# Sending the last self-attention heads out in two halves of the rows, in a one-core transformer layer

## The reference, cut to what matters

```python
xn1 = _ln(x, g1, be1)
sa = _mha(xn1, xn1, Wq_s, ..., causal=True)      # 16 heads of 16 channels
x = x + (sa @ W1 + b1)
xn2 = _ln(x, g2, be2)
ca = _mha(xn2, encoder_out, Wq_c, ..., causal=False)   # 77 keys
x = x + (ca @ W2 + b2)
xn3 = _ln(x, g3, be3)
return x + relu(xn3 @ Wf1 + bf1) @ Wf2 + bf2
```

## Time and profile before

| | us |
|---|---|
| median of 3 runs (590.23 to 590.74) | 590.23 |
| profiled execution | 590.62 |
| its span | 588.7 |

### The profile page before, as it was taken

How to read it: one execution, slowest core, us unless ns; L and a number is a source line. 1 busy time by engine, 2 the same in 40 slices (tenths; PEclk the granted TensorE clock), 3 DMA queues, 4 the chain that set the end, 5 groups by cost and what they waited for, 6 DMA issues and landing times.

```text
span 588.7 us, 8826 instructions
## 1 busy us (share of the span) xinstructions
PE 486.3 (83%) x3296; PEld 283.9 (48%) x3296; DVE 335.5 (57%) x645; ACT 316.0 (54%) x622; POOL 189.5 (32%) x291
## 2 busy tenths in 40 slices
PE   1588974999999999989988888685359697999887
PEld 1475651343434444444433243441226177888877
DVE  3165885877878787867863054254625285363340
ACT  3685320667676767645566667264034981445360
POOL 2497970121212121221322333216511192030200
PEclk9998997999999999989999899787559987999999
DMA  8145946025253435340121944316741520101001
GB/s 285 56 135 177 223 126 110 0 37 94 57 99 65 76 64 100 65 68 3 34 59 55 195 112 79 75 40 186 123 92 23 137 68 0 37 1 37 19 18 37
DMA packets 31370, 48.12 MB, mean 82 GB/s; under 512 B 8928, under 2 KB 25824, under 8 KB 29408
## 3 DMA queue, kind: packets, MB, share of 16 engines
q1 hardware_dynamic: 31260, 47.54, 34.9%
q10 hardware_dynamic: 68, 0.02, 0.0%
HBM read 30.66 MB, written 12.03 MB: 73 GB/s over the span
## 4 chain that ended last, share of the span: by engine, by line
PE 56%; DVE 12%; DMA 10%; ACT 10%; SPq 3%; issue 3%; POOL 2%; ACTq 0%; DVEq 0%
PE ps L1227 12%; PE ps L1075 11%; PE ps L1143 9%; PE ps L1196 9%; PE ps L1308 6%; DVE max_a L1385 4%; ACT arena_p L943 4%; PE ps L1165 4%; DMA stacks<-qc_parts 3%; DMA recips<-recip_rows 3%; PE ps L1061 2%; DVE hid_r L1488 2%; PE ps L1182 2%; PE ps L1147 2%; ACT xn L986 2%
## 5 line engine op out<-in xcount | busy, mean ns | idle before, releaser
L943 ACT ACTIVATE arena_p<-ps 128x512 f32<-128x512 f32 (+4 forms) x416 | 191.1, 543 | 151.6 <-PE ps L1196 150.7
L1385 DVE TENSOR_REDUCE max_a<-ps 128x1 f32<-128x512 f32 (+4 forms) x280 | 158.6, 620 | 70.8 <-PE ps L1143 58.7
L1143 PE MATMUL ps<-stacks 96*128 96x77 bf16 (+4 forms) x640 | 138.4, 291 | 31.1 <-DVE max_a L1385 11.3
L1196 PE MATMUL ps<-stacks 99*128 99x512 bf16 (+1 forms) x448 | 140.9, 346 | 19.1 <-DMA stacks<-shift_t 8.6
L1143 PEld LDWEIGHTS ps<-stacks 96*128 96x128 bf16 x640 | 55.0, 105 | 95.6 <-DVE max_a L1385 38.7
L1227 PE MATMUL ps<-arena_p,v_group 128*32 128x512 f32 (+3 forms) x896 | 92.9, 527 | 0.3 <-POOL arena_p L807 0.3
L807 POOL TENSOR_SCALAR_AFFINE_SELECT arena_p<-arena_p 128x512 f32<-128x512 f32 x64 | 39.9, 635 | 161.5 <-ACT arena_p L943 161.4
L1196 PEld LDWEIGHTS ps<-stacks 99*128 99x128 bf16 x448 | 42.0, 99 | 80.7 <-ACT arena_p L943 36.2
L1385 DVE TENSOR_REDUCE max_b<-ps 128x1 f32<-128x384 f32 (+3 forms) x88 | 52.9, 636 | 22.4 <-PE ps L1147 22.1
L1075 PE MATMUL ps<-wf2r,hid_r 128*128 128x256 f32 x384 | 47.1, 284 | 4.9 <-DVE hid_r L1488 3.8
L746 POOL TENSOR_TENSOR xs<-xs,row 128x256 f32<-128x256 f32 x48 | 39.6, 859 | 33.3 <-DVE xn L1342 33.3
(11 more groups left out here) (79 smaller groups left out, 505.0 us busy)
## 6 DMA issues: line engine op xcount, KB each, us to landing
arena_h<-out_t SPq DMA_DIRECT2D x16, 256.0 KB, 4.5
recips<-recip_rows SPq DMA_DIRECT2D x8, 512.0 KB
q_parts<-parts SPq DMA_DIRECT2D x8, 384.0 KB, 2.6
k_parts<-parts SPq DMA_DIRECT2D x8, 384.0 KB, 2.9
stacks<-q_parts SPq DMA_DIRECT2D x7, 384.0 KB, 5.5
stacks<-k_parts SPq DMA_DIRECT2D x7, 384.0 KB, 7.8
qc_parts<-parts SPq DMA_DIRECT2D x6, 384.0 KB, 3.5
stacks<-qc_parts SPq DMA_DIRECT2D x6, 384.0 KB, 6.8
```

The lines of the kernel that those rows point to most:

```text
L943: nc.scalar.activation(probs[0:a.kp, a.probs_slot(g, ui), h, k * BANK:k * BANK + width], ps[0:a.kp, unit % S_BANKS, 0:width], ACT.Exp, sca ...
L1143: ins = nc.tensor.matmul(m_bank(use)[:, o:o + w], q_columns(a, g, ROWS, h, t * P, (t + 1) * P), k_self[0:ROWS, slot, h, s0:s0 + w] if a.causal
L1196: ins = nc.tensor.matmul(ps[:, unit % S_BANKS, lo - k * BANK:hi - k * BANK], k_rows(a, ROWS_S, g, h, i * P), q_columns(a, g, ROWS_S, h, q0 ...
L1385: nc.vector.tensor_reduce(dst, m_bank(use)[:, 0:nh * w].rearrange("p (h w) -> p h w", h=nh), AX.X, ALU.max).then_inc(use_read, 1)
```

## The change

Self group 7 leaves in two halves of 512 rows. Piece 3 of its product, which completes bank 6, moves from -2.84 to -5.0; the first copy follows at -4.5, its DMAs at -4.0; the second copy is at +2.4 behind the last piece at +2.0 (was +2.9). Each half has its own reciprocal, store, spread (256 KB) and division, with four new semaphores; the halves of `sums` are laid out apart, so group 6's sums go by two DMAs. The rest of the list is laid anew: rows of chunk 2 come at +10 and of chunk 3 at +16, each with its own norm, turn and projection; loads, "packed", "bias", and "inverted" and "spread" of C3 get other places, "weights" becomes two steps behind the chunks of C4 and C5, and all that stood from +58 on stands 15 earlier.

```diff
+BANK_DONE = 3
+    early = ("product", SELF, NG - 1, BANK_DONE)
+    events = [(END - 5.0, 2, early) if e[2] == early else e for e in events]
-    crossed = [END + t for t in (0.0, 6.5, 13.5, 20.1, 58.0, 64.5, 74.0, 80.5)]
+    crossed = [END + t for t in (0.0, 6.5, 13.5, 20.1, 43.0, 49.5, 59.0, 65.5)]
-    add(END + 2.9, "product", SELF, NG - 1, SELF.n_pieces - 1)
+    add(END + 2.0, "product", SELF, NG - 1, SELF.n_pieces - 1)
+    for half, copied, inverted, divided in ((0, -4.5, 0.5, 7.0), (1, 2.4, 7.1, 15.0)):
+        add(END + copied, "copy", SELF, NG - 1, half)
+        add(END + copied + 0.5, "packed", SELF, NG - 1, half)
+        add(END + inverted, "inverted", SELF, NG - 1, half)
+        add(END + inverted + 0.1, "stored", SELF, NG - 1, half)
+        add(END + inverted + 0.1, "spread", SELF, NG - 1, half)
+        add(END + divided, "divided", SELF, NG - 1, half)
+    copied = {(1, 1): END + 16.5, (3, 0): END + 28.5, (3, 1): END + 30.0}
+    packed = {1: END + 16.6, 2: END + 27.2, 3: END + 30.1}
-    add(END + 51.9, "inverted", CROSS, 3)
-    add(END + 53.4, "spread", CROSS, 3)
-    add(END + 67.0, "divided", CROSS, 3)
+    for g, inverted, spread, divided in ((1, 17.5, 17.7, 31.9), (3, 39.0, 44.0, 52.0)):
+        ...
-    for n, t in enumerate([5.2 * SELF_US, 5.8 * SELF_US, END + 17.0, END + 17.1]):
+    for n, t in enumerate([5.2 * SELF_US, 5.8 * SELF_US, END + 10.0, END + 16.0]):
...
-        add((t + 6.0, t + 6.0, END + 18.0, END + 19.0)[n], "norm", SELF, n)
-    for n, t in enumerate([6.25 * SELF_US, 6.6 * SELF_US, END + 21.0, END + 23.0]):
+        add((t + 6.0, t + 6.0, END + 13.0, END + 19.0)[n], "norm", SELF, n)
+    for n, t in enumerate([6.25 * SELF_US, 6.6 * SELF_US, END + 15.2, END + 21.5]):
...
-            add(t + 3.0 + 1.0 * hh, "qproj", SELF, n, hh)
-            add(t + 5.0 + 1.0 * hh, "second", SELF, n, hh)
-    for n, t in enumerate([END + 9.0, END + 13.0, END + 32.0, END + 32.1]):
+            add(t + (3.0 if n < 2 else 2.2) + 1.0 * hh, "qproj", SELF, n, hh)
+            add(t + (5.0 if n < 2 else 4.2) + 1.0 * hh, "second", SELF, n, hh)
+    for n, t in enumerate([END + 8.0, END + 12.0, END + 28.0, END + 28.1]):
         add(t, "bias", SELF, n)
-    for g, half, t in ((4, 0, 27.5), (5, 0, 28.5), (4, 1, 31.5), (5, 1, 31.55), (6, None, 31.6), (7, None, 53.5)):
+    for g, half, t in ((4, 0, 21.0), (5, 0, 21.1), (4, 1, 27.0), (5, 1, 27.1), (6, None, 30.2), (7, None, 38.4)):
-    w2 = END + 70.0
+    w2 = END + 55.0
-    add(END + 32.2, "weights", SELF, 0)
-    add(END + 75.0, "raw", SELF, 0)
+    add(END + 36.6, "weights", SELF, 0)
+    add(END + 42.6, "weights", SELF, 1)
+    add(END + 60.0, "raw", SELF, 0)
@@ pack_sums; pack_heads takes lo:hi of the rows in the same way
+            if a.causal and g >= NG - 2:
+                for k in range(2) if half is None else [half]:
+                    eng.dma_start(sums_half[r0:r0 + GW, k, :],
+                                  out_t[1::2 * D, g % 2, k * CHUNK:(k + 1) * CHUNK]
+                                  .rearrange("h (s c) -> h s c", c=sums_half.shape[2]))\
+                        .then_inc(s.late_sums if half else s.sums_in[g % 2], 16)
+                return
@@ spread_recips
+                sp.dma_start(recips[:, lo:hi],
+                             src.rearrange("h (o t) -> h o t", o=1).to_broadcast([2 * GH, D, hi - lo]))\
+                    .then_inc(s.late_recips if half else s.recips_in, 16)
@@ copy_out
+                halves = a.n_copies if g < NG - 1 else 2
+                act.wait_ge(pv, a.pieces_to(g, BANK_DONE + 1 if a.causal and halves == 2 and n == 0
+                                            else (n + 1) * a.n_pieces // halves))
@@ rows (PE)
-                pe.wait_ge(of[a].heads_done, KC * (b + 1))
+                pe.wait_ge(of[a].heads_done, KC * (b + 1) + (a.causal and n == 3))
@@ divide_heads
+                lo, hi = (0, T) if half is None else (half * CHUNK, (half + 1) * CHUNK)
+                o = heads_out[:, g // 2, lo:hi]
+                nc.vector.tensor_tensor(o, o, recips[:, lo:hi], ALU.mult).then_inc(s.heads_done, 1)
```

More of the change, by code:

```diff
@@ L212, in add @@
         events.append((t, 3, what))
-    add(END + 2.9, "product", SELF, NG - 1, SELF.n_pieces - 1)
[L215 to L218, removed]
-        if g % 2:
[L220 to L224, removed]
+    add(END + 2.0, "product", SELF, NG - 1, SELF.n_pieces - 1)
+    for g in range(NG - 1):
+        after = starts[g + 1]
+        add(after + 5.4, "copy", SELF, g, 0)
+        add(after + 5.5, "packed", SELF, g, None)
+        if g % 2:
+            add(after + 10.1, "inverted", SELF, g, None)
+            add(after + 10.2, "stored", SELF, g, None)
+            add(after + 10.2, "spread", SELF, g, None)
+            add(after + 18.9, "divided", SELF, g, None)
+    for half, copied, inverted, divided in ((0, -4.5, 0.5, 7.0), (1, 2.4, 7.1, 15.0)):
[5 more added lines that the diff above has]
+        add(END + divided, "divided", SELF, NG - 1, half)
     for g in range(NG):
@@ L335, in build @@
         sums = sb("sums", [P, 2 * GH * T // P])
+        sums_half = sums[:, :].rearrange("p (k c) -> p k c", k=2)
         n_qkv, n_ctx = KC * 3 * C, KC * 2 * C
@@ L818, in attention @@
                         add_bias(NCH + what[0])
+                    elif op == "weights" and what[0] == 0:
+                        pool.wait_ge(ff_in, 16)
+                        pool.tensor_copy(wf1r[0], wf1).then_inc(wf1_halves, 1)
                     elif op == "weights":
-                        pool.wait_ge(ff_in, 16)
-                        weight_halves(*wf1r, wf1, wf1_halves)
+                        pool.wait_ge(wf1_halves, 1)
+                        pool.tensor_tensor(wf1r[1], wf1, wf1r[0], ALU.subtract).then_inc(wf1_halves, 1)
                     elif op == "second":
@@ L1217, in product @@
                     else:
[L1218 removed]
+                        pe.wait_ge(of[a.before].out_copied, NG * a.before.n_copies + 1)
                 slot = a.probs_slot(g, ui)
@@ L1408, in rows, with invert_sums, divide_heads @@
                     ln_sums(norm)
-            def invert_sums(a, g):
-                for p in range(2):
-                    dve.wait_ge(of[a].sums_in[p], 16 * (g // 2 + 1))
-                nc.vector.reciprocal(sums[:, :], sums[:, :]).then_inc(of[a].recips_done, 1)
-            def divide_heads(a, g):
-                dve.wait_ge(of[a].recips_in, 16 * (g // 2 + 1))
-                for p in range(2):
-                    dve.wait_ge(of[a].heads_in[p], 16 * (g // 2 + 1))
-                o = heads_out[:, g // 2, :]
-                nc.vector.tensor_tensor(o, o, recips[:, :], ALU.mult).then_inc(of[a].heads_done, 1)
+            def invert_sums(a, g, half=None):
+                if half:
+                    dve.wait_ge(of[a].late_sums, 16)
+                else:
+                    for p in range(2):
+                        dve.wait_ge(of[a].sums_in[p], 16 * (g // 2 + 1 + (half == 0 and p == 0)))
+                to = sums[:, :] if half is None else sums_half[:, half, :]
+                nc.vector.reciprocal(to, to).then_inc(of[a].recips_done, 1)
+            def divide_heads(a, g, half=None):
+                s = of[a]
+                if half:
+                    dve.wait_ge(s.late_recips, 16)
+                    dve.wait_ge(s.late_heads, 16)
+                else:
+                    dve.wait_ge(s.recips_in, 16 * (g // 2 + 1))
+                    for p in range(2):
+                        dve.wait_ge(s.heads_in[p], 16 * (g // 2 + 1))
+                lo, hi = (0, T) if half is None else (half * CHUNK, (half + 1) * CHUNK)
+                o = heads_out[:, g // 2, lo:hi]
+                nc.vector.tensor_tensor(o, o, recips[:, lo:hi], ALU.mult).then_inc(s.heads_done, 1)
             def attention(lo, hi=None):
```

79 lines of the change are left out of this document (46 added, 33 removed).

## The result

The changed kernel takes **587.57 us** (median of 6 runs, 586.54 to 588.23), beside 591.19 (590.23 to 593.77) of the kernel before: a ratio of 0.9931 [0.9906, 0.9956]. It is faster, by 3.6 us and not by the 12.9 of the forecast, and the time lies outside the range of 571 to 585. The profiled execution took 586.54 us (span 584.6) against 590.62.

A forecast was written before the change was run, and what follows sets the result against it. PE's waits behind the q projections, ended by landings of q parts, sums and q stacks, were taken as the bound. Savings of 2.3 + 3.2 + 2.9 - 1.5 + 6.0 = 12.9 us gave 577.3 us, range 571 to 585.

The forecast's parts named there:

- Rows, norm and projection: Chunk 2 and 3 rows up to the store of their parts: store 2.3 us earlier, 3 lost to 6 won.
- Arriving: First half's store 2.3 us and 256 KB spread 5.0 us after self attention: divided by 366.3; second half at 374.4.
- Weights behind the split: POOL's "weights" moved behind C4's split, so the split can follow its last maximum at once: 3.2 us won.
- Shift's copy: DVE's copy of C4's shift moved ahead of "inverted C3", which waited for sums: 2.9 us won.
- Load 6: Before C4's first score: issued at 412.6, lands 8.2 us later at 420.8; takes back 1.5 us, 0 to 4.8.
- Load 7: Issued earlier, behind C4's shift, so C4's first product no longer waits for it: 6.0 us won, or 3.3.
- Spread C3: Spread of C3's reciprocals, behind load 7 and C5's shift on SP, lands at 431.5: cost 0, up to 3.
- Feed-forward: Behind C4's first product all goes unchanged in the old order: 31.4 us, then feed-forward 117.6 us.
- signs of being wrong: Load 6 landing after 424, a wait for spread C3 over 3 us, or a longer feed-forward.
- The void halves: Rival: half a spread takes nearly as long as the whole; 580.0, or 582.6 with 3 us lost; chance 0.14.
- The DMA bound: Rival: DMA engines bound the stretch behind 403; load 6 takes 11.5 us, 5 lost together, 582.3; chance 0.17.
- The slower rival: Rival: first spread, behind load C3 on its queue, lands late and holds DVE and PE; 593 if at 382; chance 0.04.

The follow-up runs named there:

- after_warm: Changed kernel plus useless fp32 products on PE, 3 ahead of C3's third chunk step and 5 ahead of turn 2: 584.91 us, 0.9916.
- rows3_early: Changed kernel with the second half's division and chunk 3's rows moved ahead of norm 2 and turn 2: 591.07 us, 0.9985.
- halves_fixed_warm: Changed kernel with rows3_early, norm 3 ahead of the splits, first C4 and C5 loads behind the parts' stores, useless products at three places: 581.66 us, 0.9867.
- norm2_first: Changed kernel with norm 2 moved from +13 to +10.06, ahead of C3's last maxima and C3's split: 589.70 us, 0.9988.
- halves_reordered: Changed kernel with rows3_early, norm 3 ahead of the splits, and the second-half loads of C4 and C5, load 6, load 7 and spread C3 moved: 593.87 us, 1.0042.
- head_only: Changed kernel with the halves kept but the new order behind the store of the parts undone: 596.11 us, 1.0103 against the kernel before.
- tail_load7_late: tail_only with load 7 on SP behind the spread of C3, so also behind C5's shift: 590.51 us, 1.001.
- the second part: The change's new order behind the store of the parts, without the halves; alone on the kernel before: 581.79 us, 0.9864.
- tail_only: Kernel before with only the new order behind the store of the parts, group 7 leaving whole: 581.79 us, 0.9864.
- tail_load6: tail_only with load 6 ahead of packed C2 and C3, load 7 behind C3's reciprocals' store, spread C3 ahead of C5's shift: 587.25 us, 0.9913.
- piece3_back: Changed kernel with piece 3 of group 7's product behind the last exponentials again and the first copy at -2.3: 587.95 us, 0.9954.

## Why the prediction failed

**The step that failed is "Rows, norm and projection"**: the store of chunk 3's parts was to come 2.3 us earlier, between 3 lost and 6 won; it came 4.9 later, outside its bounds. That is 7.2 of the 9.6 us by which the stage misses the 12.9. By the forecast's own marks (what is off grows along the way; the changed kernel's trace runs 0.8 us ahead of that of the kernel before, so in R each is 0.8 later still):

| mark | forecast | measured |
|---|---|---|
| first half inverted, divided | 358.4, 366.3 | 358.42, 366.58 |
| rows of chunk 2 | 367.7 to 371.2 | 368.84 to 373.69 |
| norm 2, turn 2 | 378.8, 380.2 | 381.05, 382.57 |
| rows of chunk 3 | 382.4 to 385.9 | 386.83 to 391.16 |
| chunk 3's projection | 396.0 | 402.72 |
| store | 403.1 | 409.59 |

- *Arriving* was right, in part by luck. The store of the reciprocals took 3.33 us for 2.3, the spread of 256 KB 4.42 for 5.0, and the two nearly cancel. The forecast had taken 5.0 as a middle, from no row; that half the bytes take little more than half of 7.71 us bears it out. The Trainium skill (DMA: Bandwidth & Descriptors, "Anatomy of one DMA — SWDGE (gpsimd) path") puts a fixed 2.0 us and the bytes at 436 GB/s; by that, an estimate, half the spread saves 0.6 us. The trace has 3.3, so the measurement decides against using it here. That section fits DMAs of the path that GpSimd serves, and this spread is issued by SyncE, on the queue that the profile calls hardware_dynamic: no run here tests the fit on its own path.
- *PE's clock.* The forecast priced both "rows" at the full-clock 1.89 us per half and booked 1.1 us as won, since it read the block before as run at half clock. That reading was wrong: behind its wait the block ran at the lower level only for its first 2.9 us.

```profile
375.70:378.60 2.90, 2.90 (x7) 2.34 (x8) 0.00 (x0) 0.00 (x0) 0.00 (x0) 0.50 0.12 13
378.60:384.40 5.80, 5.80 (x28) 4.89 (x27) 3.74 (x11) 0.00 (x0) 0.72 (x2) 0.98 0.00 0
```

  That loss, some 1.1 us for the whole, is now met twice: the halves put a wait ahead of the first rows and a second, behind norm 2, ahead of turn 2. Rows 2, turn 2, C3's product (1.94 us for 1.06) and rows 3 cost 1.3, 0.9, 0.9 and 0.8 us more. That the clock does this is shown by `after_warm`, where norm 3 comes 4.0 us earlier. Its store, though, came only 1.3 us earlier, so the clock of these steps by itself does not bring the forecast's 2.3 us back.
- *Order on DVE.* Norm 3 was seen to stand behind both splits, and got no price of its own. It took 3.16 us where norm 2 took 1.38, beside POOL's 2.31 us of L791. `rows3_early` shows that the splits, not the rows, hold it, and only with norm 3 ahead of the splits, SP's loads behind the stores and the clock kept up together did the store come 7.7 us earlier (`halves_fixed_warm`); their shares were not taken apart. That POOL is what stretches the norm is argued from the two standing side by side (in `norm2_first` it was POOL's L782, 2.91 us, beside 3.00; with no such instruction of POOL beside it norm 3 took 1.38 in `halves_reordered`), and was not isolated.
- *Why the halves lose* is argued from the traces. In one block norm 2 and norm 3 follow each other, and one wait serves both. In halves the path goes wait, rows, wait, turn, rows, splits, wait, norm, and its end is set by chunk 3, whose heads come no earlier: this much the forecast said itself, and `head_only` (+1.0%) prices it, with the third wait at the lower clock in its profile.

**Behind the store**, term by term:

- *Weights behind the split, 3.2*: from the chunk to the split 5.86 us became 2.78, right. The maximum that had taken 3.27 us beside POOL's 4.50 takes 0.17.
- *Shift's copy, 2.9*: from the split to the copy 4.99 became 2.02, right.
- *Load 6, -1.5 (0 to 4.8)*: -4.2. It was issued 8.9 us behind the store (forecast 9.5) and its first chunk began 9.4 after that (8.2). What the forecast did not have is that C4's shift rows, issued at 421.71, stand in the same queue behind it: they landed at 428.93. From the copy to the score 3.36 became 7.52. A part of it is load 7 right behind them, as `tail_load7_late` shows.
- *No term, +1.0*: the parts landed 2.53 us after their issue for 3.43.
- *Load 7, 6.0*: 11.96 became 4.79, so 7.2. `tail_load7_late` says more: as long as load 7 is late, what the weights and the shift win does not reach the first product. They do not add to it; they wait for it.
- *Spread C3, 0 (up to 3)*: DVE waited 2.31 us; from first product to "rows" it is 0.9 us longer. A further 1.0 us between there and feed-forward is not explained; one profile's scatter is as large.
- *Feed-forward*: 117.54 for 117.60, right.

In sum -4.9 + 1.0 + 3.1 + 3.0 - 4.2 + 7.2 - 1.9 + 0.1 = 3.3 us before rounding, the stage's difference. Of the forecast's own signs of being wrong one came: load 6's first chunk began at 427.88, the sign was 424. The wait for spread C3 and feed-forward stayed inside theirs.

**The rivals.** The void halves were nearest in kind, but stopped at 582.6, because the bound of 3 us lost was made of waits at full-clock prices. The DMA bound had what lies behind load 6 about right (4.8 us lost in all, measured 4.2), but by luck: it had load 6 take 11.5 us, the first chunk began 9.4 after the issue, and the rest is the shift rows. It was wrong on load 7, for which PE did not wait. The slower rival named the wrong place: the first spread landed in time. Its price fell due at norm and turn instead.

## What to carry to other kernels

Before a block is cut in two, count the waits on its path, not the work in it: each half needs its own statistics, root and turn, and behind two of the three waits here PE began at half clock (0.50), which cost 0.8 to 1.3 us for each step there. When several savings lie ahead of one late transfer, first take the transfer away and price the others against it; with load 7 behind the spread the second part gave nothing, with it early 1.4%. On one queue a small transfer issued behind a large load takes the load's time, so the order of issues decides which of the small ones stands still.

## What the runs showed of the hardware

- **Granted clock.** From 416 to 428 us of the changed kernel PE was busy for 4.58 of 12 us and the granted clock was 0.50, the 1.2 GHz level; through the useless products of `after_warm` it was 1.00 (366 to 371), and two halves of rows took 3.62 to 3.72 us for 4.3 to 5.2. After a wait of 2.98 us it was 1.00 in the changed kernel and 0.50 in `after_warm` and `head_only`. Six useless products (5.5 us of PE, in time in which it had nothing) won 2.4 us over `tail_only` by the ratios (3.7 in the profile; the intervals overlap), and twelve more lost 3.1.
- **The queue.** The shift rows of C4 (three DMAs of 8 KB) were there 1.9 us after their last issue began in the kernel before, where load 6 had long been issued, and 6.0 us after it right behind load 6 and with load 7 right behind them; without load 7 there it was at most 3.8 (`tail_load7_late`). C5's took 7.35 us behind load 7 and a spread (`tail_load6`). The 32 KB store of reciprocals took 1.8 to 2.6 us in five kernels with one block, and 5.05 us 1.9 us behind the issue of load C3 (`piece3_back`).
- **DVE beside POOL.** The same norm (4 instructions of 128x256) took 1.35 to 1.38 us alone and 3.00 to 3.16 beside a TENSOR_TENSOR of POOL; a TENSOR_TENSOR of 16 columns on DVE 0.17 and 3.27. Which kinds of POOL instruction do this was not tried.
